# A deformable convolution in split products, its first two stages in one block, and the count and bias of finished sums on two engines

## The reference

```python
offset = jnp.clip(_conv(x, off_w, off_b), -max_off, max_off)      # 3x3, 18 channels
mask = 2.0 * jax.nn.sigmoid(_conv(x, mask_w, mask_b))             # 3x3, 9 channels
y = _deform_conv(x, offset, mask, proj_w, proj_b)                 # 9 taps, 384 -> 384 channels
mean, var = y.mean(axis=(0, 2, 3)), y.var(axis=(0, 2, 3))         # over all images
return gelu((y - mean) * rsqrt(var + 1e-5) * gamma + beta)        # and x is added to it
```

## Time and profile before

| | us |
|---|---|
| three runs, median (lowest to highest) | 3640.66 (3639.73 to 3643.25) |
| the profiled execution | 3633.77 |
| its span, first to last instruction | 3631.9 |
| offsets and table, from the start to | 197 |
| convolution, to | 1560 |
| batch norm, to about | 1640 |
| block attention, to about | 2416 |
| head attention, to the end | 3632 |

### The profile page before, as it was taken

One profiled execution on the slowest core, in us unless ns is written; L12 is line 12 of the kernel. 1 busy time (PEld: TensorE's weight loads), 2 busy tenths in 40 slices (PEclk: granted clock), 3 DMA queues, 4 the chain that ended last, 5 costly groups with the idle time before them and its releaser, 6 DMA issues. The chain is left out here.

```text
span 3631.9 us, 61742 instructions
## 1 busy us (share of the span) xinstructions
PE 3319.3 (91%) x18158; PEld 1918.7 (53%) x18158; DVE 2724.7 (75%) x5169; ACT 2247.5 (62%) x5370; POOL 1437.1 (40%) x1536
## 2 busy tenths in 40 slices
PE   7979999999999999968999999968888988889897
PEld 3434444444444444457888888844444444444443
DVE  4468888888878888876888888845677677776766
ACT  4334444444444444455777777746878777787785
POOL 2144444444444444352222222221154454544635
PEclk9989999999999999988999999978999999999998
DMA  7689989899989899741000000011322322232221
GB/s 278 234 318 345 334 336 351 325 334 334 350 329 346 337 343 338 294 175 40 17 17 17 15 17 17 17 60 45 91 73 61 88 83 65 79 91 63 58 67 56
DMA packets 213319, 621.10 MB, mean 171 GB/s; under 512 B 30848, under 2 KB 110720, under 8 KB 212736
## 3 DMA queue, kind: packets, MB, share of 16 engines
q0 software_dynamic: 82944, 453.02, 33.4%
q1 hardware_dynamic: 130176, 165.91, 14.7%
HBM read 520.21 MB, written 53.18 MB: 158 GB/s over the span
## 5 line engine op out<-in xcount | busy, mean ns | idle before, releaser
L705 PE MATMUL b_acc<-b_sampled,b_w 128*128 128x512 f32 x2592 | 1210.7, 594 | 0.0
L640 DVE SCALAR_TENSOR_TENSOR b_mix<-shared,b_weight,b_mix 128x384 f32<-128x384 f32 x864 | 532.0, 621 | 137.6 <-ACT b_mix L663 81.9
L672 ACT ACTIVATE b_sampled<-b_tps 128x384 f32<-128x384 f32 x576 | 282.1, 490 | 567.2 <-PE b_tps L723 567.1
L705 PEld LDWEIGHTS b_acc<-b_sampled,b_w 128*128 128x128 f32 x2592 | 449.3, 191 | 347.5 <-issue 347.5
L1988 DVE TENSOR_REDUCE e_neg_top<-e_next 128x1 f32<-128x1024 f32 x384 | 469.7, 1224 | 191.4 <-PE e_next L2301 163.6
L640 DVE SCALAR_TENSOR_TENSOR b_mix<-b_got,b_weight,b_mix 128x384 f32<-128x384 f32 x864 | 530.8, 620 | 91.9 <-ACT b_mix L663 55.3
L2155 ACT ACTIVATE e_prob<-e_s 128x512 f32<-128x512 f32 x768 | 416.3, 598 | 125.7 <-PE e_s L2313 124.6
L2140 ACT ACTIVATE e_unused<-e_next,e_neg_top 128x1024 bf16<-128x1024 f32 x384 | 430.2, 1120 | 99.2 <-DVE e_neg_top L1988 99.2
L596 POOL DMA_INDIRECT shared<-pair_table,b_index x288 | 293.9, 1020 | 416.9 <-DVE b_mix L640 325.9
L596 POOL DMA_INDIRECT b_got<-pair_table,b_index x288 | 291.4, 1012 | 357.3 <-DVE b_mix L640 300.4
L723 PEld LDWEIGHTS b_tps<-ident,b_mix 128*128 128x128 f32 x1728 | 223.0, 142 | 368.3 <-issue 322.8
(11 more groups left out here) (230 smaller groups left out, 5366.0 us busy)
## 6 DMA issues: line engine op xcount, KB each, us to landing
pair_table<-y SPq DMA_DIRECT2D x16, 1536.0 KB, 11.3
e_stack<-e_high SPq DMA_DIRECT2D x384, 64.0 KB, 2.0
shared<-in_x SPq DMA_DIRECT2D x8, 1536.0 KB, 7.5
shared<-in_x SPq DMA_DIRECT2D x16, 768.0 KB, 5.8
tokens<-y SPq DMA_DIRECT2D x64, 192.0 KB, 1.9
e_tok<-tokens SPq DMA_DIRECT2D x8, 1536.0 KB, 7.9
e_stack<-e_low SPq DMA_DIRECT2D x192, 64.0 KB, 2.0
shared<-tokens SPq DMA_DIRECT2D x8, 1536.0 KB, 7.3
```

What stands on the lines that cost most here:

```text
L640: ins = nc.vector.scalar_tensor_tensor(dst[:], src[:, q * C:(q + 1) * C], weight[g][:, q, k, i:i + 1], dst[:], ALU.mult, ALU.add)
L672: nc.scalar.activation(sampled[s % 2][:, :, i * P:(i + 1) * P], tps[t % 2][:, 0:C].rearrange("p (o q) -> p o q", q=P), ACT.Copy).then_inc( ...
L705: last = nc.tensor.matmul(acc[g][co][:], w_conv[:, k, ci, co * P:(co + 1) * P], sampled[s % 2][:, ci], start=(k == 0 and ci == 0), stop=(k ...
```

## The change

1. **Products.** Weights and blends are split into a high part (type fp32r) and the rest, the low part. A product becomes three: high x high, low weight x high, high x low, so a step has 27 instead of 9, spread as 6, 7, 7 and 7.
2. **The low part of the blend.** ScalarE copies the turned blend out as the high part (`high`). PE then multiplies it by minus identity and adds it to the bank (`take_high`), so the bank holds what is left, and ScalarE copies that out as the low part (`low`). PE issues `take_high` for a tile behind the transposes of the next tile, and the bank is free only after `low`.
3. **The weights** are split in the first stage: per tap one ScalarE copy and one VectorE subtraction, in images 2 to 6.
4. **Bias and count.** ScalarE adds the bias (`take`), VectorE takes the statistics (`count`), one of a group's three channel chunks per tile.
5. **One block.** The first two stages share a block. The places of the first image are loaded while image 5 is in work, the first two gathers go out when the last image is padded, and two blends are done before the last image's places.
6. **Memory.** The sums of the first six images go through one buffer to DRAM (`spill`); the last two images stay in SBUF. Batch norm starts with those two and loads the other twelve halves back (`load_y`).

Loops over the images of the first stage are written out, and so are the first and the last images of the convolution.

```diff
+                for n in range(BATCH):
+                    if n + 2 < BATCH:
+                        load_x(n + 2)
+                    write_table(n)
+                    if n:
+                        keep_places(n - 1)
+                    if n == GATHER_AT:
+
+                        sp.wait_ge(places_written[0], 32 + 1)
+                        sp.nop(nofuse=True)
+                        for g in range(2):
+                            load_places(0, g)
+                keep_places(LAST)
...
+                for n in range(BATCH):
+                    for g in range(2):
+                        if 2 * n + g and (2 * n + g - 1) // 2 < SPILLED:
+                            spill(*divmod(2 * n + g - 1, 2))
+                        if n + 1 < BATCH:
+
+                            sp.wait_ge(mixed, TURN * n + TURN // 2 * (g + 1) + SLOTS)
+                            sp.nop(nofuse=True)
+                            load_places(n + 1, g)
...
+                        if first and t == 2:
+
+                            pool.wait_ge(tp_ready, TILES * BATCH)
+                            pool.wait_ge(padded, BATCH)
+                        if first and t == 6:
+                            pool.wait_ge(off_ready, BATCH)
...
+                def low_weights(n):
+                    for k in W_AT.get(n, ()):
+                        dve.wait_ge(w_highs, k + 1)
+                        nc.vector.tensor_tensor(w_low[:, k], w_raw[:, k], w_high[:, k], ALU.subtract).then_inc(w_lows, 1)
...
+                def count(n, g, o, spilled):
+
+                    dve.wait_ge(y_staged, 2 * n + g + 1)
+                    src = staged if spilled else kept[:, 2 * (n - SPILLED) + g]
+                    ins = nc.vector.bn_stats(conv_stats[:, o, bass.ds(2 * n + g, 1)], src[:, o])
+                    if o == CH - 1:
+                        ins.then_inc(counted, 1)
...
+                    statistics(n)
+                    places(n - 2)
+                    norm(n)
+                    low_weights(n - 1)
+                places(LAST - 1)
+                dve.wait_ge(w_loaded, 32)
+                for t in range(AHEAD):
+                    blend(0, t)
+                places(LAST)
+                blends(0, start=AHEAD, first=True)
+                with dve.Fori(1, SPILLED) as n:
+                    blends(n)
+                blends(SPILLED, this=False)
...
+                def high_weights(n):
+                    for k in W_AT.get(n, ()):
+                        act.wait_ge(w_loaded, 32)
+                        nc.scalar.activation(w_high[:, k], w_raw[:, k], ACT.Copy).then_inc(w_highs, 1)
...
+                def high(n, t):
+
+                    s, i = divmod(t, GROUP)
+                    if i == 0:
+                        act.wait_ge(sampled_free, STEPS * n + s + 1)
+                    act.wait_ge(transposed, TURN * n + t + MIXES + 1)
+                    nc.scalar.activation(here(s_high, s, i), tps[t % 2][:, 0:C].rearrange("p (o q) -> p o q", q=P),
+                                         ACT.Copy).then_inc(highs_made, 1)
+
+                def low(n, t):
+
+                    s, i = divmod(t, GROUP)
+                    act.wait_ge(high_taken, TURN * n + t + 1)
+                    nc.scalar.activation(here(s_low, s, i), tps[t % 2][:, 0:C].rearrange("p (o q) -> p o q", q=P),
+                                         ACT.Copy).then_inc(lows_made, 1)
+
+                def take(n, g, o, spilled):
+
+                    act.wait_ge(acc_ready, 2 * n + g + 1)
+                    if spilled and not (isinstance(n, int) and n == 0 and g == 0):
+                        act.wait_ge(y_spilled, 32 * n + 16 * g)
+                        act.wait_ge(counted, 2 * n + g)
+                    dst = staged if spilled else kept[:, 2 * (n - SPILLED) + g]
+                    ins = nc.scalar.activation(dst[:, o], acc[g][o][:], ACT.Identity, bias=b_conv[:, o:o + 1])
+                    if o == CH - 1:
+                        ins.then_inc(y_staged, 1)
...
+                        high(n, t)
+                        if t:
+                            low(n, t - 1)
...
+                conv_parts(LAST)
+                for t in range(AHEAD):
+                    begin(0, t)
+                masks(LAST)
+                turn(0, first=True)
...
+                def turn_mix(n, t):
+
+                    pe.wait_ge(mixed, TURN * n + t + SLOTS + 1)
+                    pe.wait_ge(lows_made, TURN * n + t + 1)
...
+                    pe.wait_ge(highs_made, TURN * n + t + 1)
+                    nc.tensor.matmul(tps[t % 2][:, 0:C], minus_ident[:], s_high[s % 2][:, :, i * P:(i + 1) * P],
+                                     start=False, stop=True, skip_group_check=True).then_inc(high_taken, 1)
...
-                    pairs = [(co, ci) for co in range(CH) for ci in range(CH)]
-                    for co, ci in pairs[i * CH * CH // GROUP:(i + 1) * CH * CH // GROUP]:
-                        last = nc.tensor.matmul(acc[g][co][:], w_conv[:, k, ci, co * P:(co + 1) * P],
-                                                sampled[s % 2][:, ci], start=(k == 0 and ci == 0),
-                                                stop=(k == TAPS - 1 and ci == CH - 1))
...
+                    todo = [(w, x, co, ci) for w, x in ((w_high, s_high), (w_low, s_high), (w_high, s_low))
+                            for co in range(CH) for ci in range(CH)]
+                    for j in range(i * len(todo) // GROUP, (i + 1) * len(todo) // GROUP):
+                        w, x, co, ci = todo[j]
+                        if j == 2 * CH * CH:
+                            pe.wait_ge(lows_made, GROUP * (STEPS * n + s + 1) + 2)
+                        last = nc.tensor.matmul(acc[g][co][:], w[:, k, ci, co * P:(co + 1) * P], x[s % 2][:, ci],
+                                                start=(k == 0 and j < CH * CH and ci == 0),
+                                                stop=(k == TAPS - 1 and j >= 2 * CH * CH and ci == CH - 1))
...
-                            pe.wait_ge(mixed, TURN * n + t + SLOTS + 1)
-                            pe.wait_ge(tps_free, TURN * n + t + 1)
-                            for o in range(CH):
-                                last = nc.tensor.transpose(tps[t % 2][:, o * P:(o + 1) * P],
-                                                           mix[t % MIXES][:, o * P:(o + 1) * P], ident[:])
-                            last.then_inc(transposed, 1)
+                            turn_mix(n, t)
+                            if t:
+                                take_high(n, t - 1)
+                            elif not first:
+                                take_high(n - 1, TURN - 1)
...
+                pe.wait_ge(pchain, 14 * LAST + 1)
+                pe.wait_ge(w_lows, TAPS)
                 turn(0, first=True)
...
+    IMAGES = list(range(SPILLED, BATCH)) + list(range(SPILLED))
...
+                def load_y(j):
+                    if j >= HELD + SLOTS:
+                        sp.wait_ge(act_ready, j - SLOTS + 1)
+                    slot = (j - HELD) % SLOTS
+                    sp.dma_start(y_in[slot][:].rearrange("p o q -> p (o q)"), conv_out[half(j)]).then_inc(
+                        y_loaded[slot], 16)
+
+                for j in range(SLOTS):
+                    load_x(j)
+                for j in range(HELD, HELD + SLOTS):
+                    load_y(j)
+                for j in range(SLOTS, HALVES):
+                    load_x(j)
+                    if HELD + SLOTS <= j + 2 < HALVES:
+                        load_y(j + 2)
...
+                    if h >= HELD:
+                        act.wait_ge(y_loaded[(h - HELD) % SLOTS], 16 * ((h - HELD) // SLOTS + 1))
+                    src = kept[:, h] if h < HELD else y_in[(h - HELD) % SLOTS][:]
```

More of the change, by code:

```diff
@@ new lines, in count, with blends @@
+                def count(n, g, o, spilled):
[4 more added lines that the diff above has]
+                        ins.then_inc(counted, 1)
+                def blends(n, start=0, first=False, before=True, this=True):
+                    for t in range(start, TURN):
+                        blend(n, t)
+                        since = t - COUNT_AT
+                        if 0 <= since < CH and not first:
+                            count(n - 1, 1, since, before)
+                        if 0 <= since - TURN // 2 < CH:
+                            count(n, 0, since - TURN // 2, this)
```

673 lines of the change are left out of this document (314 added, 359 removed).

## The result

The changed kernel takes 3530.61 us (median of four runs, 3527.04 to 3531.63), the kernel before, beside it, 3640.19 (3639.50 to 3643.25): a ratio of 0.9696, 95% interval 0.9679 to 0.9712. Forecast were 3520.

A forecast was written before the change was run, and what follows sets the result against it. The prediction took PE to bound the convolution. Its terms -119 + 10 - 16 + 4 summed to -121 us, from 3640.7 to 3519.7, so 3520 us, with a range of 3445 to 3606.

The forecast's parts named there:

- Products: Convolution on PE: split products at 0.23 us each, plus the subtraction, cut PE's work from 1301 to 1182 us, -119.
- What must keep up at 2.05: Convolution, per tile: VectorE at 1.91, gathers 1.93 and ScalarE 1.6 us stay below PE's 2.05; low part has 0.45 us cover.
- Waits: PE's waits in the convolution: the existing 40 us stay, and six loop edges add 10 us, under 2 us an edge.
- Joined start: Start of the convolution: earlier gathers and blends bring the first product from 214.71 to about 198.4 us, -16.
- Splitting the weights: First stage, images 2 to 6: 10 us each on ScalarE and VectorE, covered by idle time, 0; uncovered, up to +10.
- End of the convolution: After the last product: three bias instructions and three counts follow, on two engines instead of one, 0 us.
- Batch norm: Batch norm stage: twelve chunks, 9.4 MB, come back from DRAM, +4 us, ends 0 and +15.
- The gathers as the bound: Convolution: gathers end at 373 GB/s, 2.17 us a tile with spills, giving 3579 us; chance 0.10.
- ScalarE's order: Convolution: begin, high and low in one ScalarE queue make a tile about 2.2 us, giving 3606; chance 0.10.
- PE far faster: Convolution: split products below 0.21 us leave VectorE as the bound at 1.91 us a tile, giving 3415; chance 0.05.
- The slower clock: Convolution: finer waits keep PE's mean clock at 0.85, its work becomes 1391 us, +209, giving 3729; chance 0.06.
- the signs that were named: Convolution: tile 2.05 to 2.15 us, PE busy over 95%, last product about 1430, first about 198, VectorE and DMA over 0.90.

The follow-up runs named there:

- the run in which it never waits: Changed kernel with convolution loops over images written out, and PE no longer waiting for its own last product of a group: 3483.45 us.
- the fp32 runs: Changed kernel with nine fp32 products a step instead of split ones: 3609.86 us with its loops, 3602.33 us with the convolution's loops written out.
- split undone: Changed kernel with nine fp32 products a step, no subtraction and no low copy, all else kept: 3609.86 us.
- only PE keeps its loop: Changed kernel with the convolution's loops of GpSimd, VectorE and ScalarE written out, PE's loop kept: 3529.68 us (one run).
- the two with two product sets: Changed kernel with 18 products a step: without the low part of the weights 3417.84 us, without the low part of the blends 3416.88 us.
- the three other kernels that keep its PE loop: Changed kernel with other engines' loops written out, 3529.68 us; with bias and count back on VectorE, 3560.38; without batch norm's reload, 3524.87.

## Why the prediction was right, point by point

**Products** (-119): right in kind, 12 too high. PE's work is 1194 us by the run in which it never waits, forecast 1182. Transposes and subtraction came out as forecast, 0.50 us a tile (0.33 + 0.17). The term that was mis-sized is the product: (1194.3 - 572 x 0.50)/3888 = 0.233 us, taken at 0.230 from the head attention. On 3888 of them 0.003 us are 12 us. The term was -107.

**What must keep up at 2.05:** right. VectorE and the gathers were put at 1.91 and 1.93; with less on PE they run at about 1.94. The cover of the low part held: ScalarE waits 1.1 us in all for PE's subtraction, and no row has PE waiting for the low part.

**Waits** (+10): the sum was near by luck, as its parts were not. They went from 1340.6 - 1301 = 40 to 1240.4 - 1194 = 46, +6. Under this lie two things that the prediction did not see, and they go in opposite directions. The jumps cost 38 us instead of about 10 (the fp32 runs), where it allowed under 2 us an edge more: it priced VectorE's stop alone, at six edges, while VectorE jumps at four in the changed kernel and PE's own jump became the long one. And the row of six instructions on VectorE, 14 us of the 40 that "stay", was gone. It had the move of bias and count only as a change of VectorE's mean load, 0.06 us a tile; what counted was that the six came in one piece.

**Joined start** (-16): -15.4. **Splitting the weights** (0): the first product came 0.95 us later than forecast, so that next to nothing was uncovered. **End of the convolution** (0): from the last product to the next stage it is about half a microsecond shorter.

**Batch norm** (+4): +5.5, all of it the reload.

The sum of the measured terms is -107 + 6 - 15.4 - 0.5 + 5.5 = -111, against 110 by the medians (3640.19 to 3530.61). The span of the profiled executions fell by 102.5 only: the head attention was 6.7 us longer in the second one, by no doing of the change, as its spread in the other runs shows.

**The rivals.** *The gathers as the bound:* out, 416 GB/s; the limit of about 358 that the Trainium skill states (DMA: Bandwidth & Descriptors, Specifications) does not hold in these runs. *ScalarE's order:* out, as a copy less on ScalarE changed nothing. *PE far faster:* out; 0.233 us a product, not the 0.131 of the Trainium skill (TensorE: Matmul & The Clock Gate, Back-to-back issue gap), with new weights each time. *The slower clock:* out as a mean, 0.99 through the convolution; but its mechanism is there in small, behind every loop edge.

Of the signs that were named, the tile of 2.05 to 2.15 us is 2.17 with the edges and 2.09 without (1240.4/572 and 1194.3/572), the last product ended at 1440 instead of 1430, and PE was busy for 97% of the stretch. VectorE, which was to be over 0.90, was busy for 0.86 of it (1072.57 of 1247 us).

## What to carry to other kernels

When the engine that bounds a loop gets less work, look for what it stood on in the old slack: a row of side instructions in one piece cost 14 us before and 28 afterwards, and the other engines' jumps at a loop's end some 10 and then 20. Look at the bounding engine's own jump as well: its record went from 0.2 us with nine fp32 products a step to 4.3 and more with 27 split ones. Write such loops out where the program has room for it, and spread side work one instruction a turn. Before arithmetic is moved to GpSimd, look whether VectorE reads two inputs from SBUF at the same time, and price VectorE's instructions at that.

## What the runs showed of the hardware that was not expected

- Behind a stop PE often went on at the lower clock level for several microseconds, even behind a stop of 1.83 us: the stretch behind the last edge of the changed kernel has a clock of 0.59.

```profile
1281.00:1284.00 3.00, 3.00 (x11) 2.30 (x12) 1.02 (x2) 1.37 (x3) 0.93 (x1) 0.59 0.98 387
```

- Neither the kind of product nor the length of the stop decides that alone. With fp32 products the clock stayed at 1.00 behind a stop of 2.05 us (the first row, split undone) and, in the kernel before, behind one of 2.68 (the row from 709.6 us above), but fell to 0.51 in the same kernel behind one of 2.63 (the second row). With split products it stayed at 1.00 behind a stop of 3.26 us (the third row, only PE keeps its loop). What decides it is open.

```profile
687.70:692.00 4.30, 4.29 (x15) 2.16 (x16) 3.79 (x7) 2.38 (x5) 2.30 (x2) 1.00 0.40 108
```

```profile
1046.10:1049.50 3.40, 3.40 (x7) 1.85 (x8) 3.26 (x6) 1.11 (x2) 2.14 (x2) 0.51 0.25 79
```

```profile
966.40:972.00 5.60, 5.60 (x30) 4.74 (x31) 3.44 (x6) 3.77 (x9) 0.90 (x1) 1.00 0.82 326
```

- A jump back of PE takes 0.21 to 0.23 us in the two kernels with fp32 products that keep the loop and in the two with two product sets, but 4.3 to 7.9 in the change and in the three other kernels that keep its PE loop.
- A split product of 512 columns takes 0.233 us at a clock of 1.00, half an fp32 product's record 0.215, and the order of banks makes no difference. What the 0.018 us are is open; the time of a weight load (0.188 to 0.194 us by its group) is shorter than either.
- A blend on VectorE stands still for the whole of a GpSimd subtraction: 1.70 us instead of 0.617.
